# A fused attention and feed-forward kernel: a third PSUM bank for the projections, another order of the weight splits on GpSimd, and shorter low-part score matmuls

## The chip, the cores and the metric

One NeuronCore of one Trainium2 chip runs the whole program. The metric is the device time of one execution in microseconds (us), the median of several runs. One execution is also recorded by the hardware profiler; its rows are quoted below. The engines are TensorE (PE; its weight loads are shown apart as PEld), VectorE (DVE), ScalarE (ACT), GpSimd (POOL) and SyncE (SP), which only issues DMAs here.

## What is computed

The input x is 8 sequences of 256 tokens with 512 features, so 2048 tokens. Everything is float32.

```python
qkv = layernorm(x) @ w_qkv              # 32 query heads, 8 k and v heads, D = 128
scores = einsum('bqhgd,bkhd->bhgqk', q, k) * D ** -0.5
bias = -slopes * sqrt(rel)              # rel = query - key; -inf where rel < 0
attn = softmax(scores + bias)
x = x + einsum('bhgqk,bkhd->bqhgd', attn, v) @ w_o
y = layernorm(x)
hits = softmax(y @ centroids.T / 0.1) > 0.01
dense = y @ weight.T + b_ffn
x = x + where(any hit of the query & cluster of the row hit by any query, dense, 0)
```

## The kernel before

**Units.** The attention is cut into 32 units: 8 key/value heads (a group g has 4 query heads) times 4 quads of 512 tokens (two sequences). Unit u is group u // 4, quad u % 4. `body(u, ...)` exists once on each engine, and the code on each engine is written out by hand in the order in which that engine runs it; semaphores tie the engines together. In `body(u)` TensorE projects q, k and v of unit u and, interleaved with this, finishes unit u - 1: `apply_v` (probabilities times v, in six chunks 0 to 5) and `project_out` (times w_o, four outputs 0 to 3). Units 1 and 2, and units 3 to 29, are hardware loops; units 0, 30 and 31 and the tail (what is left of unit 31, and the feed-forward of the last two quads) are written out.

**Three passes.** Each float32 product is made from a high part (rounded to fp32r, TensorE's faster float32 form) and a low part: high times high, high times low, low times high. ACT writes the high part of what comes out of PSUM, DVE subtracts it to get the low part. For weights POOL does both: `split` (lines 439 and 441) reads the float32 weights in `raw`, writes `_hi` and `_lo`, and `load_after` issues the DMA that fills the half of `raw` that has come free (two DMAs for a row block of w_qkv, lines 446 and 447; one for w_o, line 450).

**Projections.** `project(u, i)` for i = 0 to 5 makes k, the four q heads and v: 12 matmuls of 128x512 each, all from line 1133 (`three_pass`). Its result goes to PSUM bank `PJ[i % 2]`. ACT (`proj_hi`) and DVE (`proj_lo`, lines 804 for kT and 807 for qT) read it there. So from i = 2 on TensorE waits until DVE has read output i - 2 of the same bank:

```python
if i < 2:
    if attn:
        pe.wait_ge(added, u * QTILES + i - 1)
else:
    pe.wait_ge(qk_lo_done, u * 5 + i - 1)
```

`project_out` uses the same two banks afterwards. Bank `TR[1]` is free in most of a body: it holds a score bank in unit 0 and some feed-forward results near the end.

**Probabilities.** DVE adds the bias and takes the row maximum (`add_bias`, lines 855 and 862), ACT takes the exponential (line 623), DVE multiplies by the reciprocal of the row sum (`normalise`, lines 871 and 875) and rearranges a chunk in 32x32 blocks (`turn`, line 825). SP writes the chunk to DRAM and reads it back transposed. ACT then makes `pT_hi` (line 612) and POOL makes the low part (`pT_lo_part`, line 480, written to `ring`); `apply_v` waits for it.

**Scores.** `scores(u, i)`, i = 0 to 7, covers two heads of one sequence and one query tile of 128. In query tile 0 (i = 0, 1, 4, 5) only the first 128 keys matter. There both q parts are multiplied by high k and low k side by side (256 columns, lines 1212 and 1213), and `add_bias` adds up the two halves of the result.

**POOL's order.** Per group, POOL splits the four row blocks of the next w_qkv after the last projection of the old group, then signals `wqkv_ready`; in unit 4g + 1 it splits w_o of the group, once unit 4g - 1's last `project_out` is through (`wo_mm`), then signals `wo_ready` (line 506), which `project_out(u, 0)` awaits. The chunks' `pT_lo_part` stand between these.

Of the kernel before, what the change touches and what calls it, by code (L numbers as in the profile page):

```python
# [43 lines left out]
def build(nc, x_in, w_qkv, w_o, w_ffn, b_ffn, cents, assign, out):  # L44
    ctx = ExitStack()
    with ctx:
        def sem(name):
            return ctx.enter_context(nc.semaphore(name))
# [96 lines left out]
        raw_split = sem("raw_split")  # L145
        wqkv_ready = sem("wqkv_ready")
        wo_ready = sem("wo_ready")
# [86 lines left out]
        def own_banks(L):  # L234

            return isinstance(L, int) and L in (0, 1, 6, 7)

        def ln_bank(L, j):
# [180 lines left out]
        def _(pool):  # L419
# [42 lines left out]
            def split_qkv(g):  # L462
                for c in range(NC):

                    pool.wait_ge(raw_loaded[c % 2], g * 96 - 96 + 32 * (c // 2 + 1))
                    split(raw[:, c % 2, :], wqkv_hi[:, c, :], wqkv_lo[:, c, :], g * (2 * NC) + SETUP + c + 1)
                    load_after(g, c)
                pool.sem_inc(wqkv_ready, 1)

# [17 lines left out]
            def group(g, last):  # L487
# [9 lines left out]

                pT_lo_part(u + 1, 0)
                pool.wait_ge(wo_mm, g * (4 * QUADS) + 4)
                for h, after in enumerate(((1, 2), (3,), (4,), (5,))):  # L500
                    split_o(g, h)
                    if h < 2 or not last:
                        load_after(g, NC + h)
                    if h == HPG - 1:
                        pool.wait_ge(raw_split, g * (2 * NC) + 2 * NC)
                        pool.sem_inc(wo_ready, 1)  # L506
                    for c in after:
                        pT_lo_part(u + 1, c)
                plain_body(u + 2)
# [5 lines left out]
            SETUP = 2 - NC  # L515

            for c in range(NC - 1):
                pool.wait_ge(w_hi_done, c + 1)
                split(first_raw(c), wqkv_hi[:, c, :], wqkv_lo[:, c, :], None)
            pool.wait_ge(raw_split, NC - 1)  # L520
            pool.wait_ge(w_last_lo, 1)
            pool.sem_inc(raw_split, 1)
            pool.sem_inc(wqkv_ready, 1)
            pool.wait_ge(dist_ready, 1)
# [39 lines left out]
            for j in range(TPQ):  # L564
                with_bias(1, j)
                if j == 1:
                    pT_lo_part(UNITS, 0)
            pT_lo_part(UNITS, 1)
            pT_lo_part(UNITS, 2)
            for p in range(2, QUADS):  # L570
# [5 lines left out]
        def _(act):  # L576
# [12 lines left out]
            def proj_hi(u, i):  # L589
                act.wait_ge(qkv_mm, u * PROJ_OUTS + i + 1)  # L590
                src = ps[:, PJ[i % 2], :]
                if i == 0:
# [147 lines left out]
        def _(dve):  # L740
# [59 lines left out]
            def proj_lo(u, i):  # L800
                dve.wait_ge(qkv_hi_done, u * PROJ_OUTS + i + 1)
                src = ps[:, PJ[i % 2], :]
                if i == 0:
# [109 lines left out]
            def body(u, proj, attn, L=None, quad=None, source=None, p=None):  # L913
# [52 lines left out]
                if p is not None:  # L966
                    cluster_bias(p)
                    cluster_hits(p)
                    dense_part(p, source, 0)
                if proj:  # L970
                    add_bias(u, 2)
                    add_bias(u, 3)
                    normalise(u, 0)
                    normalise(u, 1)
                    turn(u, 0)
# [150 lines left out]
        def _(pe):  # L1126
# [29 lines left out]
            def project(u, i):  # L1156
                first = is_first(u) and i == 0
                if i == 0 and not first:
                    pe.wait_ge(wqkv_ready, group_count(u))
                col = HPG * D if i == 0 else (HPG + 1) * D if i == PROJ_OUTS - 1 else (i - 1) * D  # L1160
# [4 lines left out]
                for c in range(NC):  # L1165
                    if first:
                        pe.wait_ge(*((raw_split, c + 1) if c < NC - 1 else (w_last_lo, 1)))
                    ins = three_pass(ps[:, PJ[i % 2], :], terms[c:c + 1], c == 0, c == NC - 1)
                ins.then_inc(qkv_mm, 1)
# [28 lines left out]
            def scores(u, i):  # L1198
# [7 lines left out]
                for h, col, _, _, _ in heads:  # L1206
# [3 lines left out]
                    if qt == 0:  # L1210
                        both = kT[:, 2 * b, :, :]
                        pe.matmul(dst, q_hi, both, start=True, stop=False)  # L1212
                        ins = pe.matmul(dst, q_lo, both, start=False, stop=True)  # L1213
                    else:
# [35 lines left out]
            def body(u, proj, attn, L=None, p=None):  # L1250

                for i in range(PROJ_OUTS):
                    if proj:
                        if i < 2:
                            if attn:
                                pe.wait_ge(added, u * QTILES + i - 1)
                        else:
                            pe.wait_ge(qk_lo_done, u * 5 + i - 1)
                        project(u, i)
# [14 lines left out]
                if attn:  # L1274
                    if proj:
                        pe.wait_ge(qk_lo_done, u * 5 + 5)
                    else:
                        pe.wait_ge(added, u * QTILES - 1)
# [3 lines left out]
                if proj:  # L1282
                    if not attn:
                        pe.wait_ge(qk_lo_done, 5)
                    if L is not None and attn:
# [77 lines left out]
            pe.wait_ge(dense_out, TPQ + FFN_TAIL)  # L1363
            apply_v(u, 0)
            pe.wait_ge(cl_exp_done, 3)
            transpose_probs(u, 3)
            apply_v(u, 1)
            pe.wait_ge(scores_biased, u * SCORE_BANKS)
            dense(1, 3)
            apply_v(u, 2)  # L1370
# [69 lines left out]
```

## Time and profile before

| | |
|---|---|
| device time, median of 3 runs | 1324.68 us (1323.49 to 1326.9) |
| device time of the profiled execution | 1328.74 us |
| its span | 1327.1 us |
| PE busy (matmul records) | 1280.5 us, 96% |
| PEld busy | 1068.1 us, 80% |
| DVE, ACT, POOL busy | 952.6, 619.5, 477.7 us |

Matmuls are pipelined: the record of a 128x512 matmul lasts about 0.39 us, while the next one starts about 0.23 us after it. So short stops of TensorE do not show in the matmul records, and the weight loads (PEld) show a stop as longer than it was.

### The profile page before, as it was taken

The page shows a single profiled execution, that of the slowest core. Times are in us where ns is not written, and L with a number is a line of the kernel's source. Part 1 is how long each engine was busy: PE and PEld are TensorE (multiplying, and loading weights), DVE is VectorE, ACT ScalarE, POOL GpSimd, SP SyncE. Part 2 cuts the span into 40 slices and gives each one's busy share as a digit, 9 for nine tenths or more (in the row PEclk, how much of TensorE's full clock was granted, in tenths as well). Part 3 has the DMA queues.
Part 4 walks back from the last instruction along what each step waited for, and adds up shares of the span by engine and source line. Part 5 has one row for each costly group of instructions (what it writes and reads, how often), then busy time and mean ns, then how long its engine had stood idle before and what let it go on. Part 6 is the DMA issues. An engine that isn't in the chain of part 4 may idle for free.

```text
span 1327.1 us, 22073 instructions
## 1 busy us (share of the span) xinstructions
PE 1280.5 (96%) x6294; PEld 1068.1 (80%) x6294; DVE 952.6 (72%) x2800; ACT 619.5 (47%) x1675; POOL 477.7 (36%) x444
## 2 busy tenths in 40 slices
PE   8899999999999999999999999999999999999987
PEld 7688877888878887888878888888878888887875
DVE  7888666777666677776666677666666677678687
ACT  2655444544444445444444454444444544554433
POOL 4311625216242444215252353316252263224213
PEclk8899999999999999999999999999999999999989
DMA  5411334223232333323232343323232242312003
GB/s 181 147 63 62 106 97 134 95 93 105 79 103 79 107 121 123 102 76 111 77 104 95 100 129 103 100 81 98 84 126 95 95 134 82 120 48 96 26 23 127
DMA packets 140296, 130.34 MB, mean 98 GB/s; under 512 B 7920, under 2 KB 105712, under 8 KB 140272
## 3 DMA queue, kind: packets, MB, share of 16 engines
q1 hardware_dynamic: 134448, 111.70, 25.5%
q0 software_dynamic: 5824, 18.36, 4.7%
q8 instruction: 11, 0.18, 0.1%
q14 instruction: 13, 0.11, 0.0%
HBM read 76.28 MB, written 53.74 MB: 98 GB/s over the span
## 4 chain that ended last, share of the span: by engine, by line
PE 52%; issue 22%; POOL 15%; DVE 7%; ACT 1%; POOLq 1%; DMA 1%; DVEq 0%; SPq 0%; ACTq 0%
PE ps L1133 47%; POOL ring L480 5%; POOL wqkv_lo L441 3%; POOL wo_lo L441 2%; DVE prob L875 2%; POOL wqkv_hi L439 2%; DVE prob L862 1%; PE ps L1213 1%; PE ps L1212 1%; POOL wo_hi L439 1%; PE ps L1153 1%; POOL raw L450 1%; DVE ring_whole L825 1%; PE ps L1294 1%; POOL bias L494 0%
## 5 line engine op out<-in xcount | busy, mean ns | idle before, releaser
L1133 PE MATMUL ps<-xnT,wqkv_hi 128*128 (+1 forms) x1568 | 490.2, 394 | 13.6 <-DVE qT_lo L807 10.1
L480 POOL TENSOR_TENSOR ring<-ring_whole,pT_hi 128x512 fp32r<-128x512 f32 x189 | 244.9, 1296 | 704.0 <-ACT pT_hi L612 703.5
L623 ACT ACTIVATE prob<-prob,negmax 128x128 f32<-128x128 f32 (+1 forms) x512 | 229.0, 449 | 333.7 <-DVE negmax L862 328.9
L1133 PEld LDWEIGHTS ps<-xnT,wqkv_hi 128*128 128x128 f32 x1568 | 290.2, 188 | 85.1 <-DVE qT_lo L807 17.8
L1133 PE MATMUL ps<-xnT,wqkv_lo 128*128 (+1 forms) x784 | 306.0, 390 | 0.0
L1133 PE MATMUL ps<-wo_hi,oT_hi 128*128 128x512 f32 x512 | 204.4, 399 | 7.4 <-POOLq L506 7.4
L875 DVE TENSOR_SCALAR prob<-prob,rinv 128x128 f32<-128x128 f32 (+1 forms) x512 | 201.1, 435 | 9.1
L1133 PE MATMUL ps<-wo_lo,oT_hi 128*128 128x512 f32 x512 | 200.1, 391 | 0.0
L1133 PE MATMUL ps<-wo_hi,oT_lo 128*128 128x512 f32 x512 | 199.9, 390 | 0.0
L842 DVE TENSOR_TENSOR acc<-ps,acc 128x512 f32 (+1 forms) x128 | 86.7, 677 | 153.2 <-PE ps L1133 153.2
L1133 PEld LDWEIGHTS ps<-xnT,wqkv_lo 128*128 128x128 f32 x784 | 147.6, 188 | 31.5
L807 DVE SCALAR_TENSOR_TENSOR qT_lo<-ps,qT_hi 128x512 fp32r<-128x512 f32 x128 | 86.2, 673 | 112.9 <-ACT qT_hi L601 112.8
L612 ACT ACTIVATE pT_hi<-ring_whole 128x512 fp32r<-128x512 f32 x189 | 119.3, 631 | 91.5 <-DMA ring_whole<-turned 88.7
L601 ACT ACTIVATE qT_hi<-ps 128x512 fp32r<-128x512 f32 x128 | 76.4, 597 | 152.4 <-PE ps L1133 152.3
L825 DVE STREAM_TRANSPOSE ring_whole<-prob 128x512 f32<-128x512 f32 x189 | 130.1, 701 | 12.6
L1133 PEld LDWEIGHTS ps<-wo_hi,oT_hi 128*128 128x128 f32 x512 | 96.4, 188 | 27.1 <-POOLq L506 9.9
L1133 PEld LDWEIGHTS ps<-wo_hi,oT_lo 128*128 128x128 f32 x512 | 96.1, 188 | 21.5
L1133 PEld LDWEIGHTS ps<-wo_lo,oT_hi 128*128 128x128 f32 x512 | 96.6, 189 | 16.8
L1133 PE MATMUL ps<-kT,qT_hi 128*128 128x256 f32 x512 | 96.6, 286 | 2.4 <-DVE negmax L862 1.9
L836 DVE TENSOR_TENSOR oT_lo<-ps,oT_hi 128x512 fp32r<-128x512 f32 x128 | 87.9, 687 | 14.7 <-ACT oT_hi L616 14.7
L623 ACT ACTIVATION_READ_ACCUMULATOR prob<-prob,negmax 128x1 f32 x512 | 96.7, 189 | 0.0
L862 DVE CUSTOM_DVE_ANT_0 prob<-ps,bias 128x256 f32<-128x256 f32 x256 | 93.8, 419 | 2.0 <-DVE ring_whole L825 0.2
(128 smaller groups left out, 1758.3 us busy)
## 6 DMA issues: line engine op xcount, KB each, us to landing
turned<-ring_whole SPq DMA_DIRECT2D x189, 256.0 KB, 2.0
ring_whole<-turned SPq DMA_DIRECT2D x189, 256.0 KB, 2.9
raw<-in_L_attn_w_qkv POOLq DMA_DIRECT2D x28, 256.0 KB, 3.1
raw<-in_L_attn_w_o POOLq DMA_DIRECT2D x28, 256.0 KB, 3.2
raw<-in_L_attn_w_qkv POOLq DMA_DIRECT2D x28, 128.0 KB, 3.0
acc<-in_L_attn_hidden_states SPq DMA_DIRECT2D x3, 1024.0 KB, 8.2
out<-acc SPq DMA_DIRECT2D x3, 1024.0 KB, 4.3
acc<-in_L_attn_hidden_states SPq DMA_DIRECT2D x4, 256.0 KB, 4.0
```

The source lines that it names most:

```text
L441: pool.tensor_tensor(lo, source, hi.bitcast(F32), ALU.subtract).then_inc(raw_split, 1)
L480: pool.tensor_tensor(ring_slot(c), whole_slot(c), pT_hi[:, c % 2, :].bitcast(F32), ALU.subtract).then_inc(pT_lo_done, 1)
L601: ins = act.activation(qT_hi[:, i - 1, :], src, ACT.Copy, scale=SCALE)
L612: act.activation(pT_hi[:, c % 2, :], source, ACT.Copy).then_inc(pT_hi_done, 1)
L623: ins = act.activation(s, s, ACT.Exp, bias=negmax[:, n:n + 1], scale=-1.0, accum_out=rowsum[:, n:n + 1])
L807: ins = dve.scalar_tensor_tensor(qT_lo[:, i - 1, :], src, SCALE, qT_hi[:, i - 1, :].bitcast(F32), ALU.mult, ALU.subtract)
L825: dve.transpose(whole_slot(c).rearrange("p (j h c) -> p h j c", h=HPG, c=BLK), source.rearrange("p h (j c) -> p h j c", c=BLK)).then_inc(p ...
L836: dve.tensor_tensor(oT_view(u, oT_lo, k), pv_view(u, k), oT_view(u, oT_hi, k).bitcast(F32), ALU.subtract).then_inc(oT_lo_done, 1)
L842: dve.tensor_tensor(acc[:, at], ps[:, out_bank(u, k), :], acc[:, at], ALU.add).then_inc(added, 1)
L862: ins = dve.tensor_tensor_reduce(out=s, in0=ps[:, score_bank(u, i), bank_col:bank_col + (qt + 1) * P], in1=bias[:, h, :] if qt else s, sca ...
L875: ins = dve.tensor_scalar(s, s, rinv[:, n:n + 1], None, ALU.mult)
L1133: ins = pe.matmul(dst, l, r, start=start and m == 0, stop=stop and m == n - 1)
```

## The change

Six edits:

1. Projections take three banks: output i goes to `(PJ[0], PJ[1], TR[1])[i % 3]`; in unit 0, where TR[1] holds scores, v (i = 5) goes to PJ[0]. TensorE waits for DVE's low part of output i - 3 in place of i - 2, and not at all for i = 2. The first `project_out` waits for one low part fewer, and the scores wait for the last.
2. POOL, unit 4g + 1: one `pT_lo_part` after each of the four w_o splits; the two w_qkv loads that followed the splits come after the last chunk.
3. POOL, w_qkv splits: the loads of w_o that stood between splits 2 and 3 and behind 3 both stand behind the splits; `wqkv_ready` goes, and TensorE waits for each row block in the first projection by `raw_split`.
4. Query tile 0: low q is multiplied by high k alone, 128 columns for 256.
5. Start: POOL begins the first splits only when DVE has written all four normalised tiles (`ln_ready`). In unit 0 DVE normalises and turns chunk 0 before it adds the bias of scores 2 and 3.
6. Tail: the 12 matmuls of `dense(1, 3)` move ahead of the transposes of chunk 3 and `apply_v(u, 1)`; on POOL, pT_lo_part 1 and 2 move between the `with_bias` steps.

```diff
+        def proj_bank(u, i):
+            if is_first(u) and i == PROJ_OUTS - 1:
+                return PJ[0]
+            return (PJ[0], PJ[1], TR[1])[i % 3]
...
                     split(raw[:, c % 2, :], wqkv_hi[:, c, :], wqkv_lo[:, c, :], g * (2 * NC) + SETUP + c + 1)
-                    load_after(g, c)
-                pool.sem_inc(wqkv_ready, 1)
+                    if c < 2:
+                        load_after(g, c)
+                load_after(g, 2)
+                load_after(g, 3)
...
-                pT_lo_part(u + 1, 0)
                 pool.wait_ge(wo_mm, g * (4 * QUADS) + 4)
-                for h, after in enumerate(((1, 2), (3,), (4,), (5,))):
+                for h in range(HPG):
                     split_o(g, h)
-                    if h < 2 or not last:
+                    if h < 2:
                         load_after(g, NC + h)
-                    if h == HPG - 1:
-                        pool.wait_ge(raw_split, g * (2 * NC) + 2 * NC)
-                        pool.sem_inc(wo_ready, 1)
-                    for c in after:
-                        pT_lo_part(u + 1, c)
+                    pT_lo_part(u + 1, h)
+                pool.wait_ge(raw_split, g * (2 * NC) + 2 * NC)
+                pool.sem_inc(wo_ready, 1)
+                pT_lo_part(u + 1, 4)
+                pT_lo_part(u + 1, 5)
+                if not last:
+                    load_after(g, 2 * NC - 2)
+                    load_after(g, 2 * NC - 1)
...
+            pool.wait_ge(ln_ready, TPQ)
             for c in range(NC - 1):
                 pool.wait_ge(w_hi_done, c + 1)
...
                 with_bias(1, j)
-                if j == 1:
-                    pT_lo_part(UNITS, 0)
-            pT_lo_part(UNITS, 1)
-            pT_lo_part(UNITS, 2)
+                if j > 0:
+                    pT_lo_part(UNITS, j - 1)
...
+                if is_first(u):
+                    normalise(u, 0)
+                    normalise(u, 1)
+                    turn(u, 0)
                 if proj:
                     add_bias(u, 2)
                     add_bias(u, 3)
+                if proj and not is_first(u):
                     normalise(u, 0)
                     normalise(u, 1)
                     turn(u, 0)
...
+                    elif i == 0:
+                        pe.wait_ge(raw_split, (u >> 2) * (2 * NC) + c + 1)
+                    ins = three_pass(ps[:, proj_bank(u, i), :], terms[c:c + 1], c == 0, c == NC - 1)
...
-                        ins = pe.matmul(dst, q_lo, both, start=False, stop=True)
+                        ins = pe.matmul(dst[:, 0:P], q_lo, kT[:, 2 * b, 0, :], start=False, stop=True)
...
-                        else:
-                            pe.wait_ge(qk_lo_done, u * 5 + i - 1)
+                        elif i > 2:
+                            pe.wait_ge(qk_lo_done, 4 if is_first(u) and i == PROJ_OUTS - 1 else u * 5 + i - 2)
...
-                        pe.wait_ge(qk_lo_done, u * 5 + 5)
+                        pe.wait_ge(qk_lo_done, u * 5 + 4)
...
                 if proj:
-                    if not attn:
-                        pe.wait_ge(qk_lo_done, 5)
+                    pe.wait_ge(qk_lo_done, u * 5 + 5)
...
             apply_v(u, 0)
+            pe.wait_ge(scores_biased, u * SCORE_BANKS)
+            dense(1, 3)
             pe.wait_ge(cl_exp_done, 3)
             transpose_probs(u, 3)
             apply_v(u, 1)
-            pe.wait_ge(scores_biased, u * SCORE_BANKS)
-            dense(1, 3)
             apply_v(u, 2)
```

What stands on GpSimd in unit 4g + 1 around the third and fourth w_o split, up to the signal `wo_ready`. Before (wo_lo is the end of a split, `ring` a pT_lo_part, DMA a load):

```order
L441 TENSOR_TENSOR wo_lo<-raw,wo_hi 128x512 [waits pool_step]
...
L446 DMA raw<-in_L_attn_w_qkv 128x512
...
L447 DMA raw<-in_L_attn_w_qkv 128x2x128
...
L480 TENSOR_TENSOR ring<-ring_whole,pT_hi 128x512 [waits pT_hi_done]
L439 TENSOR_SCALAR wo_hi<-raw 128x512 [waits raw_loaded1]
L441 TENSOR_TENSOR wo_lo<-raw,wo_hi 128x512 [waits pool_step]
...
L446 DMA raw<-in_L_attn_w_qkv 128x512
...
L447 DMA raw<-in_L_attn_w_qkv 128x2x128
L479 REGISTER_ALU [waits raw_split]
L480 TENSOR_TENSOR ring<-ring_whole,pT_hi 128x512 [waits pT_hi_done]
```

And now:

```order
L446 TENSOR_TENSOR wo_lo<-raw,wo_hi 128x512 [waits pool_step]
L486 REGISTER_ALU
L487 TENSOR_TENSOR ring<-ring_whole,pT_hi 128x512 [waits pT_hi_done]
L444 TENSOR_SCALAR wo_hi<-raw 128x512 [waits raw_loaded1]
L446 TENSOR_TENSOR wo_lo<-raw,wo_hi 128x512 [waits pool_step]
L486 REGISTER_ALU
L487 TENSOR_TENSOR ring<-ring_whole,pT_hi 128x512 [waits pT_hi_done]
L511 REGISTER_ALU
L486 REGISTER_ALU [waits raw_split]
L487 TENSOR_TENSOR ring<-ring_whole,pT_hi 128x512 [waits pT_hi_done]
```

The loads have gone from between the splits; the signal comes at the wait for `raw_split`, with chunk 3 ahead of it and chunks 4 and 5 behind it.

On TensorE in the tail, from `apply_v(u, 0)` of the last unit (its last row first) to `apply_v(u, 2)`; `ident,prob` is a transpose of chunk 3, `xnT x11` the rest of the 12 matmuls of `dense(1, 3)`. Before:

```order
L1133 MATMUL ps<-pT_hi,v_lo 128x512
L1176 MATMUL ps<-ident,prob 128x128 [waits probs_ready,cl_exp_done]
L1176 MATMUL ps<-ident,prob 128x128 x3
L1133 MATMUL ps<-pT_hi,v_hi 128x512 [waits oT_lo_done,pT_lo_done]
L1133 MATMUL ps<-ring,v_hi 128x512
L1133 MATMUL ps<-pT_hi,v_lo 128x512
L1133 MATMUL ps<-xnT 128x512 [waits scores_biased]
L1133 MATMUL ps<-xnT 128x512 x11
L1133 MATMUL ps<-pT_hi,v_hi 128x512 [waits pT_lo_done]
```

And now:

```order
L1145 MATMUL ps<-pT_hi,v_lo 128x512
L1145 MATMUL ps<-xnT 128x512 [waits scores_biased]
L1145 MATMUL ps<-xnT 128x512 x11
L1188 MATMUL ps<-ident,prob 128x128 [waits probs_ready,cl_exp_done]
L1188 MATMUL ps<-ident,prob 128x128 x3
L1145 MATMUL ps<-pT_hi,v_hi 128x512 [waits oT_lo_done,pT_lo_done]
L1145 MATMUL ps<-ring,v_hi 128x512
L1145 MATMUL ps<-pT_hi,v_lo 128x512
L1145 MATMUL ps<-pT_hi,v_hi 128x512 [waits pT_lo_done]
```

The dense block stands ahead of the transposes, and two steps of `apply_v` that both wait for POOL's low parts now follow each other.

## Rows read from the trace of the kernel before

**Rows 1.** By stretch: busy PE, PEld, DVE, ACT, POOL; granted clock, DMA share, GB/s
```profile
36.00:60.00 24.00, 19.03 (x95) 15.44 (x94) 19.84 (x73) 14.74 (x43) 6.07 (x6) 0.86 0.32 106
605.00:757.00 152.00, 148.99 (x732) 124.37 (x731) 104.55 (x320) 71.05 (x196) 58.50 (x54) 1.00 0.31 100
```
**Rows 2.** Waits of PE's matmuls: us in total, times, longest us
```profile
PE ps L1133 <- DVE qT_lo L807: 10.1, 11, 2.1
PE ps L1133 <- POOLq L506: 7.4, 6, 1.5
...
PE ps L1133 <- DVE kT L804: 2.5, 8, 0.8
```
**Rows 3.** The same of PE's weight loads
```profile
PEld ps L1133 <- DVE qT_lo L807: 17.8, 17, 2.5
PEld ps L1133 <- POOLq L506: 9.9, 6, 1.9
PEld ps L1133 <- DVE kT L804: 9.6, 15, 1.5
```
**Rows 4.** Timeline of PE, units 16 and 30: start us, us, what, idle before
```profile
647.48 0.28 PE L1213 MATMUL ps<-kT,qT_lo 128*128 128x256 f32 x1
647.60 0.28 PE L1212 MATMUL ps<-kT,qT_hi 128*128 128x256 f32 x1
...
648.78 0.60 PE L1294 MATMUL ps<-ident,vT 128*128 128x128 f32 x4
...
1188.41 1.00 PE L1231 MATMUL ps<-fold,vT 128*128 128x64 f32 x8
```
**Rows 5.** Timeline of PE, unit 17
```profile
672.37 0.74 PE L1133 MATMUL ps<-xnT,wqkv_hi 128*128 x2 [0.98 <-DVE qT_lo L807]
...
683.66 0.50 PE L1133 MATMUL ps<-wo_hi,oT_hi 128*128 128x512 f32 x1 [1.44 <-POOLq L506]
```
**Rows 6.** Timeline of POOL, unit 17
```profile
675.81 1.29 POOL L441 TENSOR_TENSOR wo_lo<-raw,wo_hi 128x512 fp32r<-128x512 f32 x1
...
679.09 1.30 POOL L480 TENSOR_TENSOR ring<-ring_whole,pT_hi 128x512 fp32r<-128x512 f32 x1
...
681.07 1.28 POOL L441 TENSOR_TENSOR wo_lo<-raw,wo_hi 128x512 fp32r<-128x512 f32 x1
```
**Rows 7.** Timeline of DVE, unit 17
```profile
668.88 2.02 DVE L875 TENSOR_SCALAR prob<-prob,rinv 128x256 f32<-128x256 f32 x2
```
**Rows 8.** Timeline of DVE and POOL at the start
```profile
10.13 4.57 DVE L792 TENSOR_SCALAR prob<-acc,meanvar,rs 128x512 f32<-128x512 f32 x3
10.21 3.75 POOL L441 TENSOR_TENSOR wqkv_lo<-raw,wqkv_hi 128x768 fp32r<-128x768 f32 x2 [6.82 <-ACT wqkv_hi L682]
...
14.62 0.53 DVE L792 TENSOR_SCALAR vT<-acc,meanvar,rs 128x512 f32<-128x512 f32 x1
```
**Rows 9.** Timeline of units 0 and 1, DVE and PE
```profile
43.15 0.41 DVE L862 CUSTOM_DVE_ANT_0 prob<-ps,bias 128x256 f32<-128x256 f32 x1
...
43.98 0.50 PE L1133 MATMUL ps<-kT,qT_hi 128*128 128x256 f32 x2 [0.80 <-DVE negmax L862]
...
44.53 0.16 DVE L871 RECIPROCAL rinv<-rowsum 128x2 f32<-128x2 f32 x1
...
46.58 0.42 DVE L855 TENSOR_TENSOR prob<-ps,bias 128x256 f32<-128x256 f32 x1
...
53.45 0.76 PE L1133 MATMUL ps<-pT_hi,v_hi 128*128 128x512 f32 x1 [3.05 <-POOL ring L480]
```
**Rows 10.** Timeline of the tail, PE
```profile
1263.55 0.63 PE L1176 MATMUL ps<-ident,prob 128*128 128x128 f32 x4 [2.10 <-DVE prob L875]
1266.12 0.79 PE L1133 MATMUL ps<-pT_hi,v_hi 128*128 128x512 f32 x1 [1.94 <-POOL ring L480]
...
1267.57 4.67 PE L1133 MATMUL ps<-xnT 128*128 128x512 f32 x12
```
**Rows 11.** The same stretch, POOL
```profile
1263.22 1.32 POOL L558 TENSOR_TENSOR selected<-selected,acc 128x512 f32<-128x512 f32 x1
```

More of the change, by code:

```diff
@@ L145, in build @@
         raw_split = sem("raw_split")
-        wqkv_ready = sem("wqkv_ready")
         wo_ready = sem("wo_ready")
@@ L522, in _ @@
             pool.sem_inc(raw_split, 1)
-            pool.sem_inc(wqkv_ready, 1)
             pool.wait_ge(dist_ready, 1)
@@ L590, in proj_hi @@
                 act.wait_ge(qkv_mm, u * PROJ_OUTS + i + 1)
-                src = ps[:, PJ[i % 2], :]
+                src = ps[:, proj_bank(u, i), :]
                 if i == 0:
@@ L801, in proj_lo @@
                 dve.wait_ge(qkv_hi_done, u * PROJ_OUTS + i + 1)
-                src = ps[:, PJ[i % 2], :]
+                src = ps[:, proj_bank(u, i), :]
                 if i == 0:
@@ L1157, in project @@
                 first = is_first(u) and i == 0
-                if i == 0 and not first:
-                    pe.wait_ge(wqkv_ready, group_count(u))
                 col = HPG * D if i == 0 else (HPG + 1) * D if i == PROJ_OUTS - 1 else (i - 1) * D
@@ L1167, in project @@
                         pe.wait_ge(*((raw_split, c + 1) if c < NC - 1 else (w_last_lo, 1)))
-                    ins = three_pass(ps[:, PJ[i % 2], :], terms[c:c + 1], c == 0, c == NC - 1)
+                    elif i == 0:
+                        pe.wait_ge(raw_split, (u >> 2) * (2 * NC) + c + 1)
+                    ins = three_pass(ps[:, proj_bank(u, i), :], terms[c:c + 1], c == 0, c == NC - 1)
                 ins.then_inc(qkv_mm, 1)
```

## The prediction

> **What bounds the kernel.** I read the busy time by stretches first. In a middle group of four units TensorE's matmul records fill 148.99 of 152 us at a granted clock of 1.00, DVE 104.55, POOL 58.50 [rows 1]. TensorE is the bound, and any time that it does not wait is time off the end; DVE and POOL matter only where they make it wait. So the second view is the waits of TensorE. Its matmuls lost 10.1 us on qT_lo and 2.5 us on kT_lo, the low parts that DVE reads out of the two projection banks, and 7.4 us on POOL's signal at line 506, `wo_ready` [rows 2]. The weight loads show the same waits longer: 17.8, 9.6 and 9.9 us [rows 3]. The matmul records hide a stop behind the 0.39 us that a record lasts, and the loads count some of their usual wait for the array, so what TensorE lost lies between: 12.6 to 27.4 us on the banks, 7.4 to 9.9 us on `wo_ready`. Third, the timelines of one unit, of the start and of the tail.
>
> **Edit 1, the third bank.** In unit 17 a projection stands 0.98 us for a low part [rows 5]. With three banks output i waits for the low part of i - 3. A projection takes 12 matmuls, 2.7 us at some 0.23 us each, and an `apply_v` 0.7 us, so the wait has 3.4 us more before it stops TensorE; the longest stop is 2.1 us by the matmuls and 2.5 by the loads, all under that. I take the middle of the two counts, 20.0 us, and leave 2 for stops that another release brings back: **-18 us**, between -12.6 and -27.4. `project_out(u, 0)` waits for one low part fewer. The new wait of the scores for the last low part stands about 6 us behind the end of that projection (v's projection, one `project_out`, one `apply_v`), so it costs nothing.
>
> **Edit 2, w_o.** In unit 17 POOL ends the third split at 677.10 and starts a chunk's low part at 679.09, so one w_qkv load takes 1.99 us; the chunk takes 1.30; the next split's first part 0.68 and its second 1.28 [rows 6]. The order now has two loads fewer ahead of `wo_ready`, 4.0 us, and one chunk fewer, 1.3. That is 5.3 us earlier, against a wait of 1.44 us [rows 5] plus the some 1.5 us by which TensorE comes earlier through edit 1. The stop goes: **-8.6 us** (middle of 7.4 and 9.9). The w_qkv loads move behind chunk 5; they are read only after the end of unit 4g + 3, so two units of 38 us cover them.
>
> **Edit 3, w_qkv.** No wait of PE for `wqkv_ready` stands among the waits, so I put it at 0. The two w_o loads are late by at most one split, about 3 us, and are needed a unit later. The wait per row block only makes the first projection safer when TensorE comes early.
>
> **Edit 4, narrow scores.** 8 matmuls in each of 32 units, 256, go from 256 to 128 columns. The pace of the 256-column ones is 647.60 - 647.48 = 0.12 us [rows 4]. No row has a 128-column fp32r matmul. The nearest are float32 transposes of 128 columns: four in 0.60 us of which the last record is 0.27, so 0.11 us each [rows 4]; each also loads new weights. I take 0.11: **-2.6 us** (256 x 0.01). If only columns counted, 0.06, it would be -15.4 us. On the other side, 8 records of plain float32 with 64 columns take 1.00 us, and the program has 4 such matmuls there, two records each, so 0.21 us per matmul [rows 4]: at this price the edit costs 256 x 0.09 = 23 us. The Trainium skill speaks both ways (TensorE: Matmul & The Clock Gate): its section Back-to-back issue gap gives N / 2.4 + 2.5, 56 ns at 128 columns, which as an estimate would be -16 us; its section LDWEIGHTS puts the load of 128 stationary columns at 107 ns, with which the edit would bring 3 us. The rows at 64 and 128 columns side with the load; the first rule is a rival below.
>
> **Edit 5, the start.** Three normalised tiles took DVE 4.57 us while POOL ran two splits of 3.75 us together; a fourth, alone, took 0.53 [rows 8]. With POOL held back the three take 1.6, so layernorm is done up to 3.0 us earlier, but POOL starts some 2 us later with 5.6 us of splits. Part of the gain sticks: **-1.5 us**, from -3 to +1. In unit 0 chunk 0 is turned ahead of the bias steps that ran from 43.15 to 44.53 [rows 9], so `apply_v` of unit 1, which stood 3.05 us for it, gets it 1.4 us earlier. The price is that scores 7, which waited until 43.98 for a bias step, now waits until the two `normalise` and the `turn` are through too, 2.05 us (44.53 to 46.58); the two projections of unit 1 behind it then end about when the chunk is there. Net **-1.1 us**. After the stop of 3.05 us the granted clock falls to the 1.2 GHz level for a while: the mean of this stretch is 0.86, which is worth up to 0.14 x 24 = 3.4 us [rows 1]. The new stop at the scores is nearly as long, so I count only **-1.0 us** of it.
>
> **Edit 6, the tail.** TensorE stands 2.10 us for the probabilities and 1.94 us for POOL's chunk 1, then runs the dense block at 0.39 us a matmul, 4.67 us in all [rows 10]. The block now fills the first stop. But `apply_v` of chunk 2 follows at once, and POOL does that chunk behind one more `with_bias`, whose second half alone takes 1.32 us [rows 11] and which I put at 2.0. Chunk 1 ends just ahead of 1266.12, so `with_bias` ends at 1268.1 and chunk 2, another 1.30, at 1269.4; `apply_v` 2 started behind the dense block, at about 1272.1. That is -2.7 us. A new stop of 2.7 us may bring the low clock over busier work, for which I give back 0.7: **-2.0 us**, between 0 and -4.5.
>
> **Sum.** -18 - 8.6 - 2.6 - 1.5 - 1.1 - 1.0 - 2.0 = -34.8 us. The profiled execution took 1328.74 us, 4.06 above the median of 1324.68; so 1293.9 for a like execution and 1289.9 for the median. I say **1290**; the likeliest case's own range is 1282 to 1300.
>
> **Rivals.**
> - *The stop moves to the chunks* (15%). In unit 4g + 1 POOL now runs splits and chunks without a pause, and DVE's `normalise` runs beside it. Two steps of it took 2.02 us while POOL worked on a chunk [rows 7], and rows 8 show the same effect. Then chunks 1 to 3 come late for `apply_v`, which by my count of POOL's work has under 1 us to spare. The Trainium skill (SBUF — State Buffer, section SBUF: two separate sides) says that the two engines share one port pair, which whoever starts first holds for the whole instruction; rows 8 agree. Against it: POOL is busy 38% of the time. If half of edit 1's gain and 3 us of edit 2's go back: 1290 + 9 + 3 = 1302.
> - *Columns alone set the pace of narrow matmuls* (9%): 12.8 us better, 1277. For it: the second load could hide under the matmul before. Against it: no pair of load and matmul in the rows goes under 0.10 us.
> - *Narrow fp32r matmuls run at 0.21 us* (6%): 1290 + 2.6 + 23 = 1316; together with the first rival (3%) some 1327, no change.
> - *Slower* (5%): the narrow matmul falls out of the fast float32 form, and its columns cost as the plain form's do. Doubling the columns of the 0.21 us case gives between 0.21 (load alone) and 0.42 us (columns alone), middle 0.31: 256 x 0.19 = 49 us over now, 1290 + 2.6 + 49 = 1341. It decides from a price of 0.12 + 32.2 / 256 = 0.25 us on. Against it: the operands stay fp32r, and nothing but the width changes.
> - *The banks are not what TensorE waited for* (2%): if waits for DVE stay, edit 1 brings 0: 1308. The code says otherwise, since the released instruction stands behind `qk_lo_done`.
>
> **Numbers.** My forecast has 60%. 1275 to 1308 takes in the forecast with the bounds of its terms, the first two rivals and the last. A measurement of this kernel can tell about 0.3%, 4 us, from no change. Faster: 60 + 15 + 9 + 6 + 2 = 92%; same 3%; slower 5%.
>
> **What would show it.** Right: no wait of PE for kT_lo and hardly any for qT_lo; none for the signal `wo_ready`; four units take some 147 us in place of 151; 128-column matmuls every 0.11 us; chunk 0's `apply_v` in unit 1 starts without a stop of 3 us; `apply_v` of chunk 2 in the tail stops for POOL. Wrong: PE waits for `ring` (POOL) in units 4g + 1; `normalise` longer than before; a pace of 0.2 us or more at the low q matmul; a second stretch at the low clock.

## The result, and the profile after

The changed kernel took 1313.55 us (median of 4 runs, 1312.89 to 1317.09) against 1324.5 us before: a ratio of 0.992, 95% interval 0.9898 to 0.9942. It is faster by 11 us; the forecast was 34.7 us, and the range of 1275 to 1308 did not hold the time. The profiled execution took 1317.09 us.

In the page, DVE is what grew. Its busy time went from 952.6 to 988.8 us, and the line that scales the probabilities (`normalise`) alone grew by 41.8, more than the whole. A group's row gives busy time, mean ns of one, and idle time ahead. First the page of before, then the page of after:

```profile
PE 1280.5 (96%) x6294; PEld 1068.1 (80%) x6294; DVE 952.6 (72%) x2800; ACT 619.5 (47%) x1675; POOL 477.7 (36%) x444
...
L875 DVE TENSOR_SCALAR prob<-prob,rinv 128x128 f32<-128x128 f32 (+1 forms) x512 | 201.1, 435 | 9.1
```
```profile
PE 1275.0 (97%) x6294; PEld 1072.0 (81%) x6294; DVE 988.8 (75%) x2800; ACT 611.9 (47%) x1675; POOL 478.0 (36%) x444
...
L882 DVE TENSOR_SCALAR prob<-prob,rinv 128x128 f32<-128x128 f32 (+1 forms) x512 | 242.9, 516 | 9.1
```

The waits of PE in the changed kernel (what waits, for what: us in total, times, longest):

```profile
PE ps L1145 <- DVE negmax L869: 17.7, 11, 2.7
...
PE ps L1145 <- POOL ring L487: 3.6, 3, 2.3
PE ps L1145 <- DVE qT_lo L814: 2.4, 4, 0.6
...
PE ps L1145 <- POOL wqkv_lo L446: 1.5, 1, 1.5
```

Against [rows 2] the waits for the banks (10.1 and 2.5 us) have shrunk to 2.4, and the 7.4 us for `wo_ready` are gone. In their place stands one wait that was 1.9 us in all before: 17.7 us for `negmax`, the bias step on the scores. It comes at one place of each group, the scores of unit 4g + 3, where POOL splits w_qkv for the next group. Its timeline in unit 15, before:

```profile
615.54 0.85 POOL L439 TENSOR_SCALAR wqkv_hi<-raw 128x768 fp32r<-128x768 f32 x1
616.47 1.85 POOL L441 TENSOR_TENSOR wqkv_lo<-raw,wqkv_hi 128x768 fp32r<-128x768 f32 x1
618.97 0.60 POOL L450 DMA_DIRECT2D raw<-in_L_attn_w_o  x1 [0.65 <-POOL wqkv_lo L441]
619.60 0.85 POOL L439 TENSOR_SCALAR wqkv_hi<-raw 128x768 fp32r<-128x768 f32 x1
...
616.49 2.11 DVE L875 TENSOR_SCALAR prob<-prob,rinv 128x128 f32<-128x128 f32 x2
618.71 0.48 DVE L875 TENSOR_SCALAR prob<-prob,rinv 128x128 f32<-128x128 f32 x2
```

and after:

```profile
606.25 0.84 POOL L444 TENSOR_SCALAR wqkv_hi<-raw 128x768 fp32r<-128x768 f32 x1
607.18 1.84 POOL L446 TENSOR_TENSOR wqkv_lo<-raw,wqkv_hi 128x768 fp32r<-128x768 f32 x1
608.99 0.83 POOL L444 TENSOR_SCALAR wqkv_hi<-raw 128x768 fp32r<-128x768 f32 x1
609.90 1.84 POOL L446 TENSOR_TENSOR wqkv_lo<-raw,wqkv_hi 128x768 fp32r<-128x768 f32 x1
611.69 1.25 POOL L455 DMA_DIRECT2D raw<-in_L_attn_w_o  x2
...
607.14 2.77 DVE L882 TENSOR_SCALAR prob<-prob,rinv 128x128 f32<-128x128 f32 x2
610.00 2.02 DVE L882 TENSOR_SCALAR prob<-prob,rinv 128x128 f32<-128x128 f32 x2
...
614.52 0.50 PE L1145 MATMUL ps<-kT,qT_hi 128*128 128x256 f32 x2 [2.06 <-DVE negmax L869]
```

Two `normalise` steps of 128 columns take 0.48 us when POOL leaves them alone, and 2.0 to 2.8 us beside a split; POOL's own steps take 1.84 or 1.85 us either way. Before, the first pair was held too, but the load between the third and the fourth split (0.65 us of waiting and 0.60 of issuing) let the second pair through at 0.48. Edit 3 took that load away. DVE comes out 2.2 us later, its next bias steps are late, and TensorE stands at the scores that need their bank: 1.28 us in the first of the seven groups, 2.03 to 2.06 us in the other six. In four of these six the granted clock then falls. The windows behind these four stops, then the one behind the stop of unit 15, where it stayed up, with the clock in the third column from the end:

```profile
314.00:318.00 4.00, 4.00 (x14) 3.24 (x13) 3.93 (x14) 0.81 (x4) 0.00 (x0) 0.57 0.55 181
464.00:468.00 4.00, 3.94 (x15) 3.29 (x14) 3.89 (x14) 0.96 (x5) 0.00 (x0) 0.57 0.46 160
764.00:768.00 4.00, 4.00 (x16) 3.41 (x17) 3.71 (x14) 1.61 (x8) 0.00 (x0) 0.57 0.49 169
1065.00:1069.00 4.00, 4.00 (x18) 3.68 (x18) 3.71 (x14) 1.50 (x8) 0.00 (x0) 0.58 0.46 155
617.00:621.00 4.00, 4.00 (x19) 3.28 (x18) 3.96 (x13) 1.74 (x6) 1.03 (x1) 1.00 0.56 197
```

In the kernel before, the first four windows all have 1.00 (at a time from the start, so not at quite the same work); the first of them:

```profile
314.00:318.00 4.00, 4.00 (x23) 3.42 (x23) 3.80 (x10) 1.43 (x6) 3.23 (x4) 1.00 0.13 53
```

A mean of 0.57 over 4 us can be read as the 1.2 GHz level for 3.4 us of them; by this estimate it costs 4.00 x 0.43 = 1.7 us each time. By POOL's row that scales the bias tiles, once in four units, a group takes (936.5 - 331.3) / 4 = 151.3 us before and (1076.8 - 324.6) / 5 = 150.4 after, where the forecast named 147.

### The profile page after: what moved, and what is told of

Its sections match the earlier page's. It is cut to its first block, busy times and chain, and to the rows that moved or that the text cites. A ratio compares the mean times of both kernels' runs of the same rounds, so it can differ in the third digit from the quotient of the medians.

```text
span 1315.5 us, 22154 instructions
## 1 busy us (share of the span) xinstructions
PE 1275.0 (97%) x6294; PEld 1072.0 (81%) x6294; DVE 988.8 (75%) x2800; ACT 611.9 (47%) x1675; POOL 478.0 (36%) x444
## 4 chain that ended last, share of the span: by engine, by line
PE 73%; DVE 18%; issue 6%; ACT 1%; DMA 1%; DVEq 1%; POOL 0%; SPq 0%; ACTq 0%; POOLq 0%
PE ps L1145 68%; DVE prob L882 7%; DVE prob L869 3%; PE ps L1224 2%; DVE ring_whole L832 1%; PE ps L1305 1%; DVE prob L862 1%; PE ps L1225 1%; PE ps L1165 1%; DVE stats L760 1%; DVE rinv L878 1%; DVE qT_lo L814 1%; DVE negmax L869 1%; DVE kT L811 0%; PE ps L1236 0%
## 5 line engine op out<-in xcount | busy, mean ns | idle before, releaser
L1145 PEld LDWEIGHTS ps<-xnT,wqkv_hi 128*128 128x128 f32 x1568 | 295.4, 191 | 68.4 <-DVE qT_lo L814 5.1
L882 DVE TENSOR_SCALAR prob<-prob,rinv 128x128 f32<-128x128 f32 (+1 forms) x512 | 242.9, 516 | 9.1
L832 DVE STREAM_TRANSPOSE ring_whole<-prob 128x512 f32<-128x512 f32 x189 | 130.2, 701 | 12.6
L1145 PEld LDWEIGHTS ps<-kT,qT_hi 128*128 128x128 f32 x512 | 84.6, 194 | 27.2 <-DVE negmax L869 23.0
```

The lines of the kernel that those rows point to most:

```text
L832: dve.transpose(whole_slot(c).rearrange("p (j h c) -> p h j c", h=HPG, c=BLK), source.rearrange("p h (j c) -> p h j c", c=BLK)).then_inc(p ...
L882: ins = dve.tensor_scalar(s, s, rinv[:, n:n + 1], None, ALU.mult)
L1145: ins = pe.matmul(dst, l, r, start=start and m == 0, stop=stop and m == n - 1)
```

## The experiments

Theory A after the result: edit 3 costs what is missing, through DVE; edits 1 and 2 do what the forecast said. All times are medians; the ratios are against runs of the kernel before on the same chip.

**The loads back.** Edit 3 undone as to the w_o loads, all else changed:

```diff
-                    if c < 2:
-                        load_after(g, c)
-                load_after(g, 2)
-                load_after(g, 3)
+                    load_after(g, c)
```

> The changed kernel with the two w_o loads put back between and behind the third and fourth w_qkv split, as before; all else as changed. Theory A (the splits without a pause hold the port that DVE's two normalise steps of unit 4g + 3 need, so the bias steps come late, scores 6 waits 2.2 us in each of 7 groups, and the clock falls behind it in some): the wait of PE for negmax goes from 17.7 us to under 4, the two normalise pairs from 2.8 + 2.0 us to some 2.1 + 0.5, and the time to 1292 to 1299 us. Theory B (DVE has become the bound because TensorE comes earlier through the third bank, wherever the loads stand): 1310 to 1316 us, the wait stays.

1296.77 us, ratio 0.9795 (0.9778 to 0.9811): 16.8 us better than the changed kernel. A group takes (1059.2 - 320.7) / 5 = 147.7 us, the forecast's figure. The wait for the bias steps went too, and the second pair is fast again (the waits, then DVE's timeline in unit 15). The page's `normalise` row goes from 242.9 to 213.2 us, so 29.7 of the 41.8 us that it had grown belong to edit 3; the other 12 stay:

```profile
PE ps L1142 <- DVE negmax L866: 4.2, 4, 2.7
```
```profile
599.07 2.16 DVE L879 TENSOR_SCALAR prob<-prob,rinv 128x128 f32<-128x128 f32 x2
601.33 0.48 DVE L879 TENSOR_SCALAR prob<-prob,rinv 128x128 f32<-128x128 f32 x2
```

**The loads moved, in the kernel before.**

```diff
-                    load_after(g, c)
+                    if c < 2:
+                        load_after(g, c)
+                pool.wait_ge(raw_split, g * (2 * NC) + NC)
                 pool.sem_inc(wqkv_ready, 1)
+                load_after(g, 2)
+                load_after(g, 3)
```

> The kernel before with only those two w_o loads moved behind the fourth w_qkv split (ready signal behind the last split). Theory A: normalise in unit 4g + 3 takes 4.8 us for two pairs, scores 6 waits some 2 us in 7 groups, 1338 to 1346 us. Theory B: no change, 1322 to 1327 us.

The added `wait_ge` holds the signal back until the last split is done, which the load did before. 1360.84 us, ratio 1.0276 (1.0255 to 1.0296): 37 us slower, more than theory A gave. The waits show where most of it lies (10.1 and 1.9 us in the same rows before). Not only the scores wait; the next unit's projections do too, because with two banks DVE's delay reaches TensorE a second time, through the low parts. The mean granted clock of its runs is lower too, 0.981 to 0.984 where the kernel before has 0.991 to 0.995.

```profile
PE ps L1137 <- DVE qT_lo L811: 19.1, 15, 2.0
PE ps L1137 <- DVE negmax L866: 14.9, 10, 2.0
```

**The splits after the normalising.** Is it the load that is needed, or only the gap? Here the loads stay where edit 3 put them, and POOL waits ahead of split 2 until DVE has normalised:

```diff
+                    if c == 2:
+                        pool.wait_ge(probs_ready, g * (SCORE_BANKS * QUADS) - SCORE_BANKS + 2)
```

> The changed kernel in which POOL starts the third w_qkv split only when DVE has finished the second normalise of unit 4g + 3 (one wait for probs_ready). Theory A: the normalise pairs take 0.5 us each there, no wait of scores 6, the splits still end ahead of their use, 1284 to 1293 us. Theory B: DVE is as late as before, 1310 to 1316 us. A third outcome: the last split comes late for the first projection of the next group, with PE waiting for wqkv_lo.

1299.64 us, ratio 0.9819 (0.9802 to 0.9835), 13.9 us better than the changed kernel with the loads in the same place. PE waits 5.1 us for `negmax`. In unit 15 the two pairs take 0.49 and 0.48 us. So what counts is that POOL stays off while DVE scales these two pairs, whichever way; the loads arrive even later here, and the time came back all the same. It missed theory A's range of 1284 to 1293 by 7 us and stays 2.9 us behind the kernel with the loads back. The trace shows two things that differ: in unit 15 the later splits now hold a pair of 256 columns (2.34 us, its neighbour 0.63), and PE waits for `ring` 7 times, 5.1 us in all, where the changed kernel has 3 and 3.6. That these make up the 2.9 us is not shown.

**The third bank alone** (`proj_bank` and its waits, put into the kernel before).

> The kernel before with only the third projection bank and its waits. Theory A: the bank waits go and nothing takes their place, 1304 to 1310 us (the term was -18). Theory B: the waits for the low parts turn into waits for the bias steps, 1316 to 1324 us, with over 10 us of PE waiting for negmax.

1315.83 us, ratio 0.9949 (0.9931 to 0.9966), 7.9 us of the 18. Theory A missed it, and the sign of theory B (over 10 us for `negmax`) is 1.9 us in the trace. The bank waits went as forecast, but the stop for `wo_ready`, 7.4 us in [rows 2], more than doubled: TensorE now comes to it sooner (its longest stop was 1.5 us, the one in unit 17 1.44, which is 2.71 now):

```profile
PE ps L1139 <- POOLq L512: 17.6, 7, 2.8
PE ps L1139 <- POOL ring L486: 7.2, 3, 3.2
```

**The w_o order alone** (edit 2, put into the kernel before).

> The kernel before with edit 2 alone: the new order of the w_o splits, the chunk parts and the w_o loads on GpSimd; two accumulator banks as before. It closes the square of the two edits: third bank alone 1315.8, both 1299.9. Theory A (the two only pay together, since units 4g+1 stop once for the banks and once for wo_ready): the waits for wo_ready (7.4 us on TensorE) go, the bank waits (12.6 us) stay, 1316 to 1320 us. Rival B (the terms of the prediction add up: -8.6 alone): 1315 to 1316.5. Rival C (with the bank waits left nothing is won, as the next bank wait takes up what wo_ready gave): 1321 to 1325.

1343.13 us, ratio 1.0141 (1.0124 to 1.0158): 18 us slower. No theory had that sign. In unit 17 DVE's pairs of 256 columns take 1.85 and 2.55 us beside the closer packed splits and chunks; before, the first took 1.03 and the second 2.02 [rows 7]. The first q low part then comes late for its bank. The timeline there, and the row of the waits:

```profile
669.95 1.85 DVE L877 TENSOR_SCALAR prob<-prob,rinv 128x256 f32<-128x256 f32 x2
...
671.90 2.55 DVE L877 TENSOR_SCALAR prob<-prob,rinv 128x256 f32<-128x256 f32 x2
...
675.21 0.65 DVE L809 SCALAR_TENSOR_TENSOR qT_lo<-ps,qT_hi 128x512 fp32r<-128x512 f32 x1
...
675.92 1.00 PE L1135 MATMUL ps<-xnT,wqkv_hi 128*128 x2 [2.29 <-DVE qT_lo L809]
```
```profile
PE ps L1135 <- DVE qT_lo L809: 17.5, 12, 2.6
```

With the 9.3 us for kT_lo the bank waits are 26.8 us where they were 12.6, and the 7.4 us for `wo_ready` are gone: 6.8 us more in all. The mean granted clock is lower as well, 0.983 to 0.986 in its runs where the kernel before has 0.992 to 0.994, and the profiled execution, the fastest of the four, is only 10.4 us behind the profiled one of before. How the 18 us divide between stops and clock is not settled.

**Both together** (edits 1 and 2 in the kernel before, loads of w_qkv untouched).

> The kernel before with edits 1 and 2 alone: the third bank, and the new order of the w_o splits and their loads. The four w_qkv loads stay where they were, between the splits. Theory A (the third bank moved TensorE's stop from the accumulator banks to wo_ready, since units 4g+1 came to wo_ready sooner than GpSimd did, and the w_o order is what turns the bank's gain into time; the two terms of the prediction then hold together: -18 and -8.6): 1294 to 1300 us, waits for qT_lo under 5 us in all, for wo_ready (POOLq) under 2 us. Rival B (GpSimd is late for another reason than the chunk parts between its splits): the waits for wo_ready stay above 10 us, 1307 to 1316 us. Rival C (with w_o parts of the probabilities later, their readers wait): new waits for pT_lo or ring on GpSimd of 1 to 2 us in each of eight units, 1305 to 1312 us.

1299.91 us, ratio 0.9813 (0.98 to 0.9826): 24.6 us against the 26.6 of the forecast. Theory A holds. DVE takes as long as with edit 2 alone (2.87 + 1.82 us, there 1.85 + 2.55), yet TensorE hardly stands there (0.57 us for 2.29), since with the third bank it waits for a low part later (DVE's timeline in unit 17, then the waits):

```profile
652.90 2.87 DVE L883 TENSOR_SCALAR prob<-prob,rinv 128x256 f32<-128x256 f32 x2
655.88 1.82 DVE L883 TENSOR_SCALAR prob<-prob,rinv 128x256 f32<-128x256 f32 x2
```
```profile
PE ps L1141 <- DVE qT_lo L815: 2.9, 5, 0.6
```

The four kernels make a square: 1324.5 neither, 1315.8 the bank, 1343.1 the order, 1299.9 both. Each edit removes the stop that the other one runs into.

**Narrow scores alone.**

```diff
-                        ins = pe.matmul(dst, q_lo, both, start=False, stop=True)
+                        ins = pe.matmul(dst[:, 0:P], q_lo, kT[:, 2 * b, 0, :], start=False, stop=True)
```

> The kernel before with edit 4 alone: the low query part meets only the high key part, 128 columns in place of 256, in the 256 products of query tile 0. Theory A (a pair of a wide and a narrow matmul takes 0.171 + 0.060 = 0.231 us in the changed kernel's trace, against 0.120 + 0.120 before, so 9 ns less for each narrow one): -2.3 us, 1320.5 to 1322.5. Rival B (columns alone set the time, 53 ns less each): -13 us, 1311. Rival C (a narrow matmul takes 0.21 us, as one that has to wait for its weights): +23 us, 1347. Since VectorE, not TensorE, sets the pace at places, A may also come to 0.

1323.12 us against 1324.51, ratio 0.9992 (0.9981 to 1.0003). That can't be told from no change, nor from the 2.3 us of theory A; rivals B and C are out.

**The tail, GpSimd's old order** (on the kernel with the loads back).

```diff
                 with_bias(1, j)
-                if j > 0:
-                    pT_lo_part(UNITS, j - 1)
+                if j == 1:
+                    pT_lo_part(UNITS, 0)
+            pT_lo_part(UNITS, 1)
+            pT_lo_part(UNITS, 2)
```

> The faster kernel of the first batch (the change with the w_o loads put back between the w_qkv splits, 1296.8 us) with GpSimd's old order in the tail: the bias sums of column 1 run ahead of the probability parts 1 and 2 instead of between them; TensorE's new tail order stays. Theory A (in the changed kernel GpSimd stood idle for 2.35 us before part 1 and then made two bias sums of 1.3 us between the parts, so that part 2 came 2.3 us late at TensorE and its clock fell to the lower level for 7 us behind the stop): 1292.5 to 1295 us, the wait for ring in the tail under 0.5 us. Rival B (part 1 becomes late instead): a stop of 0.8 to 2 us one product earlier, 1296 to 1298 us.

1292.65 us, ratio 0.9765 (0.9751 to 0.9779): 4.1 us better, **the fastest kernel of this study**. First the timeline of POOL and PE in the changed kernel's tail and the window from the stop on, then PE's timeline and a window across the stop of this one:

```profile
1252.31 1.27 POOL L487 TENSOR_TENSOR ring<-ring_whole,pT_hi 128x512 fp32r<-128x512 f32 x1 [2.35 <-ACT pT_hi L619]
1253.56 0.69 POOL L564 TENSOR_SCALAR selected<-bias_bc,query_sel 128x512 f32<-128x512 f32 x1
1254.34 1.26 POOL L567 TENSOR_TENSOR selected<-selected,acc 128x512 f32<-128x512 f32 x1
1255.55 1.27 POOL L487 TENSOR_TENSOR ring<-ring_whole,pT_hi 128x512 fp32r<-128x512 f32 x1
...
1256.88 0.80 PE L1145 MATMUL ps<-pT_hi,v_hi 128*128 128x512 f32 x1 [2.27 <-POOL ring L487]
```
```profile
1256.00:1262.00 6.00, 5.12 (x14) 4.15 (x15) 5.00 (x9) 2.48 (x4) 0.82 (x1) 0.51 0.00 0
```
```profile
1235.11 0.51 PE L1144 MATMUL ps<-pT_hi,v_hi 128*128 128x512 f32 x1 [0.33 <-POOL ring L484]
```
```profile
1220.00:1240.00 20.00, 18.42 (x91) 14.47 (x90) 19.31 (x53) 10.61 (x29) 7.91 (x7) 1.00 0.24 79
```

POOL had 2.35 us with nothing to do ahead of chunk 1; the new order left it idle and put a bias sum (0.69 + 1.26 us) behind it, in front of chunk 2. In the old order that sum stands in the hole. The stop of 2.27 us becomes 0.33, and the clock stays up, in the next 20 us too.

**The tail, all of edit 6 undone** (same base).

> The same faster kernel with edit 6 undone altogether, on GpSimd and on TensorE: the product of dense layer tile (1,3) stands behind the value product of chunk 1 again. The prediction's term for edit 6 was -2.0 us, so by it 1298.8 us. Theory A (from the changed kernel's trace, in which the stop moved by one chunk and kept its length): 1296 to 1298 us, with the stop of about 2 us before the value product of chunk 2 back where it was. If GpSimd's order is the part that costs and TensorE's the part that gains, this lies 1 to 2 us above the kernel with the old GpSimd order alone.

1297.76 us, ratio 0.9799 (0.9785 to 0.9812). So edit 6 is two edits of opposite sign: TensorE's new order is worth 5.1 us (1297.76 to 1292.65), more than the 1 to 2 expected of it; GpSimd's costs 4.1. Together that is 1.0, which the runs can't tell from nothing (0.9799 against 0.9795).

**Unit 0's old order, and no wait at the start** (each on the fastest kernel).

> The best kernel so far (loads put back, GpSimd's old tail order, 1292.65 us) with the old order of VectorE in unit 0: the bias sums of scores 2 and 3 ahead of the normalising of scores 0 and 1. The prediction's term for this part was -1.1 us for the wait and about -1.0 for the clock, so by it 1294 to 1295 us. Theory A (from the traces: the stop at the first value product shrank from 3.05 to 0.69 us, and a new one of 2.9 us came at scores 7 of unit 0, so the stop only moved): 1292 to 1293.5, with the 2.7 us stop at scores 7 gone and one of about 3 us at the first value product back.

> The same best kernel without edit 5, GpSimd's wait for the four normalised tiles before its first w_qkv splits. The prediction's term was -1.5 us, so by it 1294.2 us, with VectorE's three normalisings of 512 columns at 4.6 us in place of 1.46 and the projections starting at 19 instead of 14 us from the span's start. Theory A (the whole 5 us of earlier start count, less the 1.5 us stop for the third split): 1295.5 to 1297.5 us. Rival B (what is won at the start is lost to GpSimd's lateness behind it): 1291.5 to 1293 us.

1295.32 us, ratio 0.9775 (0.9759 to 0.9791), and 1294.18 us, ratio 0.9771 (0.9758 to 0.9784). The intervals overlap with that of the fastest, so these 2.7 and 1.5 us are the size of the forecast's terms (2.1 and 1.5) but are not shown, and the traces have less: TensorE's same step in unit 3, a transpose at 149.44 us in the fastest kernel, comes at 150.16 with the old order and at 149.68 without the wait, 0.7 and 0.2 us later. The rows of the first do show that the stop moves. With the new order of unit 0 TensorE stands 2.71 us at the scores and hardly at the first value product; with the old one:

```profile
41.46 0.50 PE L1139 MATMUL ps<-kT,qT_hi 128*128 128x256 f32 x2 [0.81 <-DVE negmax L868]
...
51.09 0.76 PE L1139 MATMUL ps<-pT_hi,v_hi 128*128 128x512 f32 x1 [3.20 <-DVE negmax L868]
```

Theory A for the start (3 to 5 us) fell: the first projections do begin earlier (at 14.76 us, at 17.05 without the wait), but behind them TensorE stands 1.51 us for the third split, and of the 2.3 us only 0.2 are left at the scores (43.10 and 43.29 us). That is rival B's mechanism, though the median lies above its range. Theory A for unit 0's order, 1292 to 1293.5 us, was missed by the median as well.

## Why the prediction was wrong

- **Edit 3 is the step that failed.** "No wait of PE for `wqkv_ready` stands among the waits, so I put it at 0." I asked who waits for the moved loads and found nobody. I did not ask what ran in the gap that they left. Undoing it brings 16.8 us, over two thirds of the 23.5 us between forecast and result. I had the mechanism in hand as the first rival (`normalise` beside POOL), with [rows 7] and [rows 8], and looked for it in units 4g + 1 only; the w_qkv splits of unit 4g + 3 are longer (0.84 + 1.84 us against 0.62 + 1.28) and had no rows in my working. The 2.02 us of [rows 7] themselves lay beside a chunk's low part and the first step of the split behind it, not beside a chunk alone. Between the two profiled executions lie 1317.09 - 1296.65 = 20.4 us. Of these, 2.7 us lie in each of seven groups, 18.9 in all; the rows have 13.5 us of stops there and, in four groups, some 6.8 of low clock. Most of the rest, 1.2 us, lies in the tail behind the stop for chunk 2, where the clock is low for longer in the execution of the changed kernel. Two of the forecast's own signs of being wrong had come: `normalise` longer than before, and new stretches at the low clock.
- **Edits 1 and 2** were right in size, -24.6 for -26.6, and right in mechanism. That the size came out so near is in part luck: it was the middle of two counts, and by the matmul rows alone the waits that went are 20.0 - 2.9 = 17.1 us. What the terms did not say is that they hold only as a pair. Summed one by one they would have been read as two gains; alone they measure -7.9 and +18. The forecast did count the 1.5 us by which TensorE comes earlier to `wo_ready`. Its terms left out that edit 2 delays DVE, a delay that two banks pass on; the first rival had the delay, but sought its price at the chunks.
- **Edit 4** was right. I took 0.11 us for a narrow matmul. The rows show that the width moves time within the pair, 0.06 us behind the narrow one and 0.17 behind the wide one, 0.231 for the pair where [rows 4] had 0.24:

```profile
648.02 0.22 PE L1225 MATMUL ps<-kT,qT_lo 128*128 128x128 f32 x1
648.08 0.34 PE L1224 MATMUL ps<-kT,qT_hi 128*128 128x256 f32 x1
648.25 0.22 PE L1225 MATMUL ps<-kT,qT_lo 128*128 128x128 f32 x1
```

  That is 9 ns for each of 256, 2.3 us by the rows; the time of edit 4 alone can't tell it from nothing. The weight loads start 0.11 to 0.12 us apart whichever width follows. The gap rule that the Trainium skill gives (TensorE: Matmul & The Clock Gate, Back-to-back issue gap), 56 ns, agrees with the 60 ns behind the narrow matmul, and yet gives the wrong total. The same section says that the rule is for an isolated matmul and counts too little where each has a weight load, for which it has some 81 ns at 128 columns; the working passed over that, and the pace of the loads here is slower still. Its load rule, 107 ns for 128 columns (section LDWEIGHTS), comes nearest: as an estimate 214 ns for the two loads of a pair, beside the 231 measured. That the loads set the pace fits the rows; no run tests it alone.
- **Edit 5** came out near its terms in the medians (4.2 us for 3.6), inside the noise, and that is luck: in the traces the two parts are worth 0.7 and 0.2 us by unit 3. The step that failed is "part of the gain sticks": the wait for the third split takes nearly all of it.
- **Edit 6** was forecast at -2.0 and came out at -1.0, inside the noise. The two stops of [rows 10], 2.10 and 1.94 us, became 0.84 and 2.27: the new stop that the forecast put at 2.7 us at chunk 2 is there. The -2.7 us came too: measured from the `dense` block that both kernels run just ahead of `apply_v` 0 (its start is at 1245.44 us now, 1257.86 before), `apply_v` of chunk 2 starts after 11.4 us, where it was 14.2. I gave back 0.7 us for the low clock; the window 1256 to 1262 at 0.51 costs 6 x 0.49 = 2.9 us. That POOL stood idle ahead of chunk 1, so that the old order was free, I did not see.
- **Without edit 3** the sum would have been 34.8 us for a measured 27.7; that 1296.77 us lies in the forecast's range. Besides edit 3, edits 1 and 2 lack 2.0, edit 4 about 1, edit 6 1.0; the remaining 3 us or so are not settled.

The rival "the stop moves to the chunks", at 15% and 1302 us, named the right pair of engines and the wrong place.

## What to carry to other kernels

When a DMA issue is moved, ask not only who waits for the data but which other engine worked in the pause that the issuing engine took for it: here DVE's second pair ran in that pause. Edits that each remove one of two stops close behind one another can be worth little, or less than nothing, apart; forecast and test them as a set, and look at what each delays on engines with slack. Where the other engine has a hole ahead of a late step, put work that is due anyway into it (here the bias sum ahead of chunk 1) and not behind that step.

## What the runs showed of the hardware

- Of DVE's steps of the attention only one kind was held by POOL: the scaling of float32 from SBUF to SBUF (the layernorm's was too, [rows 8]), two of 128 columns in 0.48 us alone and up to 2.77 us beside two w_qkv splits. In the changed kernel one such step takes 0.27 to 1.97 us, but the sums of 128x512 that read a PSUM bank 0.65 to 0.69 and the transposes 0.67 to 0.72 throughout; in unit 17 of the kernel before, while POOL's split of 1.28 us ran from 670.84:

```profile
671.03 0.71 DVE L825 STREAM_TRANSPOSE ring_whole<-prob 128x512 f32<-128x512 f32 x1
671.66 0.65 DVE L807 SCALAR_TENSOR_TENSOR qT_lo<-ps,qT_hi 128x512 fp32r<-128x512 f32 x1
```

  The Trainium skill (SBUF — State Buffer, section SBUF: two separate sides) says that GpSimd and a DVE step in a 2-port mode, or with two SBUF inputs, share a port pair: the one that starts first holds it for its whole instruction and the other blocks. The rows agree for DVE, whose pair in unit 15 of the kernel before ends at 618.60, 0.28 us behind POOL's step. They show besides that it is not even: POOL's steps follow each other within 0.1 us and stay at 1.84 us, while DVE gets through when POOL waits and issues a load (0.65 + 0.60 us).
- Behind a stop of 2.03 to 2.06 us the granted clock fell to the 1.2 GHz level, for some 3.4 us by the means of the windows, in four of six like places, and not in the other two; the seventh stop, 1.28 us, was not followed by it either.
